# Attention stage of a two-layer kernel: stores and late splits spread over more steps, a verdict that waits for the last split, additions in two pieces at the end, and products that nobody reads between the first row units

## The reference, cut to what matters

```python
q = x @ Wq; k = x @ Wk; v = x @ Wv
latent_kv = (k + v) @ W_down_kv
k_rec = latent_kv @ W_up_k; v_rec = latent_kv @ W_up_v
scores = jnp.einsum('bhqd,bhkd->bhqk', qh, kh) * scale
scores = jnp.clip(jnp.nan_to_num(scores, nan=-1000000000.0), -CLAMP, CLAMP)
decay = jnp.exp(-LAMBDA_DECAY * TIME_STEP * jnp.abs(idx[:, None] - idx[None, :]))
scores = scores * decay[None, None, :, :]
attn = jax.nn.softmax(scores, axis=-1)
out = jnp.einsum('bhqk,bhkd->bhqd', attn, vh)
```

## Time and profile before

| | us |
|---|---|
| median of 3 runs | 919.28 |
| lowest and highest | 917.18, 923.25 |
| the profiled execution | 915.32 |
| its span in the trace | 913.7 |
| mean granted TensorE clock | 0.873 |

### The profile page before, as it was taken

One profiled execution on the slowest core, in us unless ns is written; L12 is line 12 of the kernel. 1 busy time (PEld: TensorE's weight loads), 2 busy tenths in 40 slices (PEclk: granted clock), 3 DMA queues, 4 the chain that ended last, 5 costly groups with the idle time before them and its releaser, 6 DMA issues. The chain is left out here.

```text
span 913.7 us, 27626 instructions
## 1 busy us (share of the span) xinstructions
PE 751.8 (82%) x11563; PEld 473.8 (52%) x11563; DVE 599.5 (66%) x1370; ACT 469.5 (51%) x966; POOL 270.0 (30%) x526
## 2 busy tenths in 40 slices
PE   6699998999999999987539669999995993138990
PEld 3245565666666666654418646566663561025770
DVE  3877986898989888990642136676776445753444
ACT  4757885888888888876215343343432312011222
POOL 2566432343434343443026440000000000015630
PEclk9658997999999999999759969999997995557995
DMA  6532442322222121000771236000000004001104
GB/s 193 168 91 78 110 134 83 98 62 57 66 55 65 56 61 30 6 3 3 217 201 46 65 121 206 1 2 1 1 2 0 1 0 139 3 3 43 43 24 147
DMA packets 41612, 61.31 MB, mean 67 GB/s; under 512 B 11364, under 2 KB 22317, under 8 KB 41488
## 3 DMA queue, kind: packets, MB, share of 16 engines
q1 hardware_dynamic: 37742, 52.02, 19.2%
q0 software_dynamic: 2304, 4.74, 2.0%
q10 hardware_dynamic: 1442, 2.77, 1.0%
HBM read 44.18 MB, written 15.07 MB: 65 GB/s over the span
## 5 line engine op out<-in xcount | busy, mean ns | idle before, releaser
L932 DVE CUSTOM_DVE_ANT_0 junk<-row,rest 128x1024 bf16<-128x1024 f32 x256 | 312.6, 1225 | 53.9 <-PE row L446 36.7
L702 ACT ACTIVATE prob<-score 128x512 f32<-128x512 f32 x512 | 276.3, 596 | 74.3 <-PE score L543 73.3
L543 PE MATMUL score<-stack 75*32 75x512 bf16 (+14 forms) x3968 | 174.4, 285 | 3.9 <-issue 2.4
L840 POOL TENSOR_TENSOR prob<-prob,prob_late 32x128 f32<-32x128 f32 x256 | 115.5, 451 | 187.9 <-ACT prob L702 173.3
L572 PE MATMUL out_ps<-prob,v_aug 128*32 128x256 f32 x2048 | 161.1, 390 | 3.9 <-POOL prob L840 3.9
L446 PE MATMUL row<-stack 72*32 72x512 bf16 x1928 | 155.6, 395 | 0.0
L543 PEld LDWEIGHTS score<-stack 75*32 75x32 bf16 (+1 forms) x3968 | 106.4, 98 | 74.1 <-issue 11.5
L572 PEld LDWEIGHTS out_ps<-prob,v_aug 128*32 128x32 f32 x2048 | 65.1, 112 | 55.6 <-POOL prob L840 11.2
L1835 POOL MEMSET ones<- 128x128 bf16 x2 | 0.4, 206 | 233.6 <-POOLq L1276 214.4
L2068 PE MATMUL outs<-vm_w,mixed 128*64 128x256 f32 x512 | 61.7, 381 | 1.8 <-issue 1.8
L1549 PE MATMUL up_ps<-rows_t,up_w 128*128 128x320 f32 (+1 forms) x192 | 60.6, 443 | 1.3 <-DVE rows_t L1761 1.2
(11 more groups left out here) (304 smaller groups left out, 1008.2 us busy)
## 6 DMA issues: line engine op xcount, KB each, us to landing
stack<-parts_dram SPq DMA_DIRECT2D x32, 288.0 KB
stack<-parts_dram SPq DMA_DIRECT2D x96, 96.0 KB
parts_dram<-prob SPq DMA_DIRECT2D x12, 256.0 KB
parts_dram<-spare SPq DMA_DIRECT2D x12, 256.0 KB
results<-x_tok SPq DMA_DIRECT2D x12, 256.0 KB, 3.7
up_w<-in_L_ffn_w_dram SPq DMA_DIRECT2D x1, 2048.0 KB, 9.4
rows<-x_tok SPq DMA_DIRECT2D x8, 256.0 KB, 3.3
y<-results SPq DMA_DIRECT2D x8, 256.0 KB, 4.1
```

Of the source, the lines that this page charges most:

```text
L543: last = pe.matmul(out[c:c + SUB, a - begin:b - begin], tile[0:rows, half, 1, h, at + c:at + c + SUB], tile[0:rows, half, 0, h, a:b], star ...
L702: act.activation(prob[:, t, w * HALF:(w + 1) * HALF], score[n % NS][:, :], ACT.Exp).then_inc(score_read, 1)
L840: pool.tensor_tensor(own, own, late, ALU.add).then_inc(added, 1)
L932: dve.tensor_tensor_reduce(junk[:, slot % 2, :], row[slot % 2][:, :], rest[:, S - P - t * P:2 * S - P - t * P], 1.0, LOWEST, ALU.mult, ALU ...
```

## The change

Six things are altered, all in `attention()`:

1. PE issues 12 float32 products of 384 columns into a free buffer once its projections are done, and one more behind each of the 15 row units before step 0. Nobody reads them (`keep_clock`). The turn of head 0's maxima stands one row unit earlier (`NEG_0` -6), and the wait for the copied values stands ahead of the row units.
2. The twelve stores of the second sequence's parts go out two at a time behind the rows of maxima of heads 5 to 10 (`store_two`).
3. The rows of maxima of heads 1 and 2 are sent by SP, behind loads, and no longer by ACT.
4. The late pieces of parts, which took one step each in steps 0 to 11, stand one or two to a head up to step 42. The waits of POOL follow (`adds_done`).
5. The verdict stands at step 253, and DVE's four passes wait for the last split of maxima (`neg_chain`).
6. The last additions of the last head are made in two pieces of two tiles, at `t` 5 and 7.

```diff
+WARM = 384
+WARM_FIRST = 12
-VERDICT_AT = 5
+VERDICT_AT = 12
-        NEG_0 = -5
+        NEG_0 = -6
...
+            def store_two(n):
+                b, half, k = 1, n // (FILL // 2), 2 * (n % (FILL // 2))
+                if half:
+                    sp.wait_ge(late_part2, 4)
+                for k in range(k, k + 2):
+                    if half:
+                        send_part(sp, 1, 1, k // NPART, k % NPART, stored[1])
+                    else:
+                        store_parts(sp, 1, 0, k // NPART, k % NPART, stored[1])
...
             load_masks(sp, 0, 2, masks_in[1])
+            store_neg(sp, 1)
             sp.wait_ge(rows_set, 2)
-            for n in range(4):
-                fill_side(2, n, (6, 8, 10, 13)[n])
+            for n in range(2):
+                fill_side(2, n, 6 + 2 * n)
+            store_neg(sp, 2)
+            for n in range(2, 4):
+                fill_side(2, n, 7 + 2 * n)
...
+            def keep_clock(out):
+                pe.matmul(out, ident[:, :], x_t[:, 0:WARM], start=True, stop=True)
             pe.wait_ge(ident_cast, 1)
+            for n in range(2):
+                pe.wait_ge(raw_copied[0, n], 2)
+            for n in range(WARM_FIRST):
+                keep_clock(row[1][:, 0:WARM])
+            pe.wait_ge(v_copied, 4)
             for step in range(-LEAD, 0):
                 for kind, n in slots_at(step):
                     wide_row_unit(n)
+                    keep_clock(score[1 + n % 2][:, 0:WARM])
                 if step == NEG_0:
-                    pe.wait_ge(v_copied, 4)
                     turn_neg(0)
...
-                pe.wait_ge(added, 2 * GH * m + GH * (t // 4 + 1))
+                pe.wait_ge(added, 2 * GH * m + GH * (t // 4 + 1 + (m == NH - 1 and t >= 6)))
...
-                if 1 <= step < 5:
-                    late_first_part(step - 1)
-                if 6 <= step < 10:
-                    late_second_part(step - 6)
+                if t % 4 == 3 and 11 <= step < 27:
+                    late_first_part(step // 4 - 2)
+                if t % 4 == 3 and 27 <= step < 43:
+                    late_second_part(step // 4 - 6)
...
+                if t in ((3, 5, 7) if m == NH - 1 else (3, 7)):
+                    tiles = 2 if m == NH - 1 and t > 3 else 4
+                    first = t + 1 - tiles
...
+                if step in (2, 4, 5, 6):
+                    adds_done(step)
+                    late_scale((0, 0, 0, 0, 1, 2, 3)[step])
+                if step in (14, 18, 22, 26):
+                    adds_done(step)
+                    late_first_left((step - 14) // 4)
+                if step in (30, 34, 38, 42):
+                    adds_done(step)
+                    late_second_left((step - 30) // 4)
...
                         dve.wait_ge(row_done, slot_at["verdict", 0])
+                        dve.wait_ge(neg_chain, NEG_STEPS * NH)
                         for b in range(B):
                             for side in range(2):
                                 reach(b, side)
```

More of the change, by code:

```diff
@@ L367, in _ @@
             store_neg(sp, 6)
+            store_two(1)
             for n in range(2, 4):
-                fill_side(5, n, 39 + 2 * n)
-            for k in range(FILL):
-                store_parts(sp, 1, 0, k // NPART, k % NPART, stored[1])
+                fill_side(5, n, 41 + 2 * n)
             for pair in range(6, PAIRS + 3):
@@ L382, in _ @@
                             store_neg(sp, m)
+                            if 7 <= m < 11:
+                                store_two(m - 5)
                     if n != 2 and pair < PAIRS:
                         fill_side(pair, n, first + (0, 1, 6, 10)[n])
[L385 to L389, removed]
             for n in range(2):
@@ L822, in late_second_left, with adds_done @@
                                    ALU.subtract).then_inc(late_part2, 1)
+            def adds_done(step):
+                m, t = step // SB, step % SB
+                count = 2 * GH * m + GH * (t > 3)
+                if count:
+                    pool.wait_ge(added, count)
             for step in range(STEPS):
                 m, t = step // SB, step % SB
[L826 to L830, removed]
-                        pool.wait_ge(neg_chain, NEG_STEPS * (m + 2))
-                    if step in (15, 23):
-                        pool.wait_ge(values_set, 6 + 3 * (step == 23))
-                    pool.wait_ge(score_read, unit(m, t, w) + 1)
+                if t == 3 and m + 1 < NH:
+                    pool.wait_ge(neg_chain, NEG_STEPS * (m + 2))
+                if step in (3, 7):
+                    pool.wait_ge(late_scaled, step // 4 * 3 + 1)
+                if step in (15, 19, 23, 27):
+                    pool.wait_ge(late_left, (step - 11) // 4)
+                if step in (31, 35, 39, 43):
+                    pool.wait_ge(late_part2, (step - 27) // 4)
+                if t in ((3, 5, 7) if m == NH - 1 else (3, 7)):
+                    tiles = 2 if m == NH - 1 and t > 3 else 4
+                    first = t + 1 - tiles
+                    pool.wait_ge(score_read, unit(m, t, t // 4) + 1)
@@ L835, in _ @@
                     for c in range(GH):
-                        begin, at = w * (4 * S - HALF), w * S + c * SUB
                         of = slice(c * SUB, (c + 1) * SUB)
-                        own = prob_all[of, begin:begin + 4 * (S + P)].rearrange("p (t s) -> p t s", s=S + P)[:, :, at:at + SUB]
-                        late = prob_late[of, m % 2, 4 * w * SUB:4 * (w + 1) * SUB].rearrange("p (t s) -> p t s", s=SUB)
+                        begin = min(first * (S + P), SB * S - tiles * (S + P))
@@ L840, in _ @@
+                        at = first * (S + P) - begin + c * SUB
+                        own = prob_all[of, begin:begin + tiles * (S + P)].rearrange("p (t s) -> p t s", s=S + P)[:, :, at:at + SUB]
+                        late = prob_late[of, m % 2, first * SUB:(t + 1) * SUB].rearrange("p (t s) -> p t s", s=SUB)
                         pool.tensor_tensor(own, own, late, ALU.add).then_inc(added, 1)
```

31 lines of the change are left out of this document (10 added, 21 removed).

## The result

The changed kernel took 905.75 us (median of 4 runs, 901.51 to 906.86) against 918.8 for the kernel before (917.18 to 923.25), a ratio of 0.9851 with an interval of 0.9806 to 0.9897. The medians differ by 13.05 us, where 20.9 had been forecast as the likeliest. The span of the profiled execution is 905.0 us against 913.7, its mean granted clock 0.903 against 0.873.

The account below looks back on a forecast made before the run. PE was taken to bound the attention stage, the gain being its clock dips and a hole. Terms summed to -20.9 from the profiled 915.3, 894.4; with the median 4.0 above the profile, 898.4 us, range 893 to 909.

Parts of the forecast that it names:

- Products before the first row unit: Unread products on PE between projections and first row unit: 0 us, with an end of +1.0.
- Between row units: One unread product behind each row unit keeps DVE's pace of 1.15 us: 0, with 3 us as an end.
- The wait at step 0: PE's 0.74 us wait for head 0's maxima before step 0 goes, their turn being a unit earlier: -0.7 us.
- The clock in heads 0 and 1: With no hole on PE the clock stays up before step 0; heads 0 and 1 shorten: -9.6 us, from 0 to -10.5.
- The rival that was given 12%: Clock held up to step 0 falls in the first steps, through small PE holes; loses the 9.6: 908 us; 12%.
- Late pieces: Moved POOL pieces may delay step 7's additions; ACT's roundings move to steps with free time: +0.3 us, from 0 to +2.
- Maxima of heads 1 and 2 on SP: Head 1's row, behind step 0's loads and masks, ends about 60.5 us, needed at some 62: +0.5, 0 to +2.
- Stores in pairs: Rows of maxima no longer behind 1.5 MB of stores; heads 6 and 7 take 10.96 us each: -7.3, end 0.
- the rival of a late row (10%): A row of maxima, head 1's or one of heads 5 to 10, still comes late: 906 us; 10%.
- The verdict: Split free of DVE's passes, which now run beside head 30's additions; its first weighing comes earlier: -2.5 us.
- If the wait costs the clock as it did before, -0.5: Low end at the verdict: if PE's wait costs the clock as before, the move gives only -0.5 us.
- The last additions: Last head: two tiles weighed before the last additions, which take 1.3 us for 2.0: -1.6, from -0.9 to -1.9.

Follow-up runs that it names:

- no_warm: The changed kernel without the 27 products that nobody reads; 914.3 us, ratio 0.993 to the kernel before.
- adds_first: The changed kernel, with DVE's passes of the verdict waiting for POOL's additions of head 30; 901.68 us, ratio 0.9824 to the kernel before.
- late_back: The changed kernel with the late pieces back in steps 0 to 11; 903.31 us, ratio 0.9893 to the kernel before.
- warm_only: The kernel before with only the unread products and the earlier turn of head 0's maxima added; 921.52 us, ratio 1.0021.
- stores_back: The changed kernel with the twelve stores in two blocks of six again; 911.28 us, ratio 0.9932 to the kernel before.

## Why the prediction was right and where it was wrong

The direction, the places and most of the mechanisms were right, and the time lies in the range; the forecast of 898.4 is 7.4 us too low. That the two terms of the clock came out so close in the first pair of profiles is luck in part, since both move by 2.4 us and more between executions of one kernel. Against the first profile of before, step by step:

*Products before the first row unit:* 0 forecast, +1.0 as the end. PE's last projection started at 25.73 and the first row unit at 35.26, 9.5 us later; it was 8.8 before (25.36 and 34.16) and 8.9 in no_warm. The cost is +0.6 to +0.7. *Between row units:* 0 forecast; the pace is 1.08 to 1.14 us, which is right.

*The wait at step 0:* -0.7 forecast, with the argument that the row was late because its turn was. Measured +1.6 at the diagonal block (53.38 to 54.99). This step was wrong. The turn stands at 46.50 now, 0.5 earlier, and nothing comes of it. ACT's copy of the row waits for the stores of the second half, and SP's loads stand behind them (timeline of ACT and of SP's queue, changed kernel):

```profile
47.15 0.25 ACT L711 COPY neg_rows<-score 24x128 bf16<-24x128 bf16 x1 [1.06 <-DMA parts_dram<-prob]
```

```profile
35.30 6.52 SPq L294 DMA_DIRECT2D parts_dram<-prob  x6
47.15 0.83 SPq L114 DMA_DIRECT2D stack<-parts_dram  x1
48.02 1.41 SPq L117 DMA_DIRECT2D stack<-parts_dram  x3
```

Step 0 starts 5.7 to 6.5 us behind the issue of the last loads in four profiles (52.57 behind 46.83 before, 54.53 behind 48.02 here, 52.93 behind 46.98 in no_warm, 53.34 behind 47.53 in adds_first). Which of the row and the loads lands last the trace does not tell. But the copy began 0.26 us earlier than before (47.15 and 47.41), the last loads were issued 1.19 later, and step 0 came 1.96 later, which makes the loads the likelier gate.

*The clock in heads 0 and 1:* -9.6 forecast, and 31.1 - 21.6 = -9.5 measured in this pair. But it is that in some executions only. The rival that was given 12%, a clock that falls in the first steps, came in 3 of the 8 profiles that have both the products and the spread pieces, at a price of 3.2 to 6.4 us and not of the whole 9.6. Its reason had been sought in the small holes of steps 0 to 4; it starts right behind the wait in front of step 0, of which the forecast had said that it goes. And the kernel before varies too, 31.1 and 28.4. A slip of the working is small: 10.96 us a head is 1.37 us a step and not 1.3, and only an end of this term rests on it.

*Late pieces:* the +0.3 priced what moving them costs and missed what it may give. With the pieces left in head 0 the clock falls at 62 us and 6.3 us of the 9.5 are gone in that profile (late_back). The cost is small: heads 2 to 5, where most of the pieces now stand, take 44.9 us in place of 44.8. Another cost was not forecast: heads 8 to 29 take 247.4 us in place of 246.4. It is not that of the pieces, which end in head 5: late_back has 247.4 as well. Nor is it that of the products (warm_only has 246.4) or of the stores in pairs (stores_back has 247.4). Which of the other parts makes it is open.

*Maxima of heads 1 and 2 on SP:* +0.5 forecast, nothing seen. There is no wait for head 1's row, which SP issues at 59.07 us and head 1 uses from about 65 on. No run has this part alone. The rule of DMA: Bandwidth & Descriptors in the Trainium skill (Queues, rings and completion order), by which the prediction had the row up to 2 us late, did no harm here; that it is wrong is not shown, since the row had some 6 us.

*Stores in pairs:* -7.3 forecast, 29.2 - 22.4 = -6.8 measured in the pair, and -4.4 against the second profile of before. No first score unit waits for its row in the three profiles of the changed kernel, so the rival of a late row (10%) did not come.

*The verdict:* -2.5 forecast as the middle of -4.0 and -0.5; head 30 went from 14.13 to 13.68, -0.45, the low end. The price of the additions was right: 1.1 each had been forecast, 4.4 for four, and they took 4.55. What was wrong is that the clock was left out of the middle value. PE's first weighing came 9.50 us behind the head's first diagonal block, before 10.94, but the 3.16 us of waiting then let the clock fall at 401.9, and the time from there to the next head grew from 3.19 to 4.18. "If the wait costs the clock as it did before, -0.5" was the line that came true. The single instructions point to the mechanism: POOL's additions of 0.45 took 1.24, 1.32, 1.32 and 0.45, and the passes beside them 1.47 and 1.46 in place of 1.22, as if one addition slipped in between two passes and held the next pass up by 0.25. That agrees with the section Who interferes with whom of SBUF — State Buffer in the Trainium skill, by which the pair of ports that the two engines share is an exclusive lock.

*The last additions:* -1.6 forecast. From head 31's diagonal block to the end of the last weighing it was 13.9 us (418.99 to 432.90) and is 11.9 (405.01 to 416.90): -2.0. The additions of two tiles took 1.47 us, where 1.3 had been estimated. No run has this part alone, so the figure rests on the two profiles.

With the products' +0.7 contained in the +1.6 of step 0, and the +1.0 of heads 8 to 29, these make some -16 up to o_tok, where the two profiles are 15.9 apart, in place of -20.9. Beyond it the forecast assumed that nothing changes; that holds, but not of one execution: with the hole in the first mixture of experts in one and not in the other, the spans differ by 8.7 us and not by 15.9. Over the chips the ratios of 0.985 to 0.987 stand for 12 to 14 us, and the attention stage gives it: from the first diagonal block to o_tok it took 381.4 in the mean of two profiles of before and 369.3 in the mean of three after, 12.1 less. The terms that were off by size are thus the wait at step 0 (-0.7 forecast, +1.6), the verdict (-2.5, -0.45), and the two that were read from one execution's clock: the two dips, 2.7 and 2.4 us longer in the first profile of before than in the second, with a gain in heads 0 and 1 that shrinks by 3.2 to 6.4 us where the clock falls behind step 0.

## What to carry to other kernels

Where a clock fall is what a change is to save, its price has to be taken from more than one execution, since the same 1.5 us of waiting cost nothing in one and 3 to 6 us in the next; and what else makes PE wait in the stretch that is to be kept at full clock has to be looked for as well: the products alone held the clock up to step 0 and gave nothing that could be measured. A slow pair of passes and small instructions on DVE and POOL is not cured by moving it beside other small instructions that PE waits for: a wait that lets the additions go first gave 3.6 us where the move had given 0.5 to 1.3.

## What the runs showed of the chip

- DVE and ACT can stand together with no releaser that the trace could name, DVE for 6.2 to 7.7 us (part of it its ordinary wait for PE, mostly 2.8 in that loop) and ACT for 2.1 to 4.8, near the same place in 11 of 13 profiles, and the clock falls behind it. The cause is open. The two profiles of the kernel before, one with and one without it, differ by 5.5 us in the first mixture.
- DVE is slowed as well when its passes, which read an SBUF tile as both inputs, run beside POOL's additions: 1.47 us in place of 1.22. Beside the small instructions of the split they kept their 1.22, and only POOL was slowed, 1.07 to 1.18 in place of 0.19.
- 12 float32 products of 384 columns in a row (24 records), which nobody reads, took 7.91 us. With them and the 15 others the clock held up to step 0 in ten profiles out of ten; without them it fell before step 0, between 29.7 and 33.0 us, in three out of three.
